# Expert layers in whole fp32 products, weights of each tile from DRAM, and scores ahead of turns

## The chip, the core and the metric

The program runs on one core of one Trainium2 chip. A core has a matrix engine (TensorE, PE in the profile; its weight loads are PEld), a vector engine (DVE), an activation engine (ACT), GpSimd (POOL) and a queue engine (SP). PE writes to PSUM, from which DVE and ACT read. The metric is the device time of one execution in microseconds; lower is better.

## The reference, cut to what matters

Two batches of 2048 tokens of 128 channels go through four layers: a time-mixing layer with a feed-forward part, a ternary feed-forward layer, a state-space layer with a scan over time, and a layer of 8 experts, of which each token takes two. The last one is, for one token x with its normalised vector n:

```
logits = n @ gate_w + gate_b                 # 8 numbers
the two best experts e1, e2, and their shares by softmax
for each of the two: h = silu(n @ w1[e]) * (n @ w3[e])   # 128 -> 512
                     y = h @ w2[e]                       # 512 -> 128
out = x + layernorm(share1 * y1 + share2 * y2)
```

## The kernel before, in words

The program has four phases, one after the other. Every engine has its own stream of instructions, written out by hand; engines wait for one another by semaphores, and no scheduler moves anything. The change touches the third and the fourth phase.

**The state-space phase** (`phase_ssm`) handles 8 tiles of 512 tokens (`body(t, b)`), each in 16 states. For each state DVE multiplies (L1794, 128x1024) and scans (L1781, twice 128x512), POOL multiplies the result by a row of coefficients (`prod`, L1734), and PE adds it up (L1503). Between them this phase also prepares the weights of the experts. There are 12 pieces of 128x1024 numbers. Each is loaded (`weights`, L1387), written by ACT as fp16 (`moe_hi`, L1667), scaled by ACT (L1669), and POOL writes what the fp16 number lacks, as fp16 too (`moe_lo`, L1749).

**The last phase** (`phase_moe`) has four stages.

1. Normalising and scoring. Six of eight groups of 512 tokens are normalised in the phase before; the two late ones here (`centre` L2004, `variance` L2010, `inverse_root`, `normalise` L2322). PE makes each group's scores (`score`, L2018) and turns each group from channels by tokens to tokens by channels (`turn`, L2029), from two fp16 halves, with an identity; ACT and DVE put the rows into SBUF (`put_rows`), and SP stores them in DRAM (`moe_rows`). Scores and turns alternate on PE.
2. Routing. A chain of small instructions on DVE picks the experts (from `logits`, L2346, to `chosen`, L2376), numbers the places (`place`, L2399) and, with PE, turns them round into lists of source rows. The number of the expert of each tile comes near the end of it (`expert`, L2475 to L2481).
3. Experts. The pairs of token and expert are cut into 39 tiles of 256 rows, each tile for one expert. A tile has two units (78 in all). POOL gathers a tile's rows from DRAM (`gather`, L2261, two indirect DMAs), PE turns them (`x_turn`, L2077), DVE copies them (`take_x`, L2491), PE makes the first layer of a unit (`up`, L1998 to L2000: `product` makes three fp16 matmuls for each output of 128x256), ACT takes silu (L2215), DVE multiplies (`hid`, L2507), ACT and DVE split the hidden values into halves (L2201, L2498), and three units later PE makes the second layer (`down`, L2110 to L2112, again three fp16 matmuls). ACT copies the result (`put_y`, L2207), and POOL scatters it to DRAM (L2280, two indirect DMAs).
4. The end: SP loads the results back (`back`), DVE adds the two of each token, POOL, PE and DVE finish the norm and the sum, and SP stores.

In the experts the order on PE is `up(n)`, then at a tile's first unit `x_turn` of the next tile, then `down(n - 3)`. POOL goes tile by tile: scatter of tile i when `y_out` has come, then gather of tile i + 6 when `up` of tile i + 2 is done.

Of the kernel before, what the change touches and what calls it, by code (L numbers as in the profile page):

```python
# [12 lines left out]
P = 128  # L13
# [14 lines left out]
PIECES = E + E // 2  # L28
# [6 lines left out]
for _name, _count in (  # L35
# [11 lines left out]
         "down squaredC varianceC logC rstdC scaledC addedC w_in0 w_in1 w_high w_scaled w_low "  # L47
# [3 lines left out]
def build(nc, xT, vecs, att_w, cv_w, tern_w, hid_w, w3_w, ssm_w, dt_w, moe_w13, moe_w2, gate_w, consts, selectors, iota_c, outT,  # L51
# [3 lines left out]
    with ctx:  # L55
# [74 lines left out]

        G.moe_hi = sb("moe_hi", [P, PIECES, 2 * FFN], F16)
        G.moe_lo = sb("moe_lo", [P, PIECES, 2 * FFN], F16)
# [1165 lines left out]
def phase_ssm(nc, G):  # L1298
# [9 lines left out]
    with mem:  # L1308
# [25 lines left out]
        raw = sb("raw3", [P, 2, 2 * FFN])  # L1334
# [33 lines left out]
        def piece(t, b, k):  # L1368
            return bass.ds((t * B + b) * 2 + k, 1)

        def splits(t):
            return not (isinstance(t, int) and t == NT - 1)

# [7 lines left out]
        def _(sp):  # L1381
            sp.dma_start(G.gatew[:, :], G.gate_w).then_inc(G.gate_loaded, 16)
            w2 = G.moe_w2.rearrange("p (e u) m -> p e (u m)", e=E // 2)
            def weights(i):
                if i >= 2:
                    sp.wait_ge(S["w_low"], i - 1)
                sp.dma_start(raw[:, i % 2, :], G.moe_w13[:, i, :] if i < E else w2[:, i - E, :])\  # L1387
                  .then_inc(S[f"w_in{i % 2}"], 16)
# [13 lines left out]
            for t in range(NT):  # L1402
                for b in range(B):
                    for n in range(DST):
                        spread_C(t, b, n)
                        if t == 0 and b == 0 and n in (1, 2):
                            weights(n - 1)
                        if n in (9, 13):
                            i = at(t, b) * 2 + (9, 13).index(n)
                            if i < PIECES:  # L1410
                                weights(i)
                        if n == 12 and not (t == NT - 1 and b == B - 1):
                            rows_out(*after(t, b))

# [138 lines left out]
        def _(act):  # L1553
# [93 lines left out]
            def body(t, b):  # L1647
                for n in range(DST):
# [16 lines left out]
            def split_weights(t, b, k):  # L1665
                act.wait_ge(S[f"w_in{k}"], at(t, b) * 16)
                nc.scalar.activation(G.moe_hi[:, piece(t, b, k), :].rearrange("p a m -> p (a m)"), raw[:, k, :], ACT.Copy,  # L1667
                                     scale=WS).then_inc(S["w_high"], 1)
                nc.scalar.activation(raw[:, k, :], raw[:, k, :], ACT.Copy, scale=WS).then_inc(S["w_scaled"], 1)  # L1669
# [21 lines left out]
        def _(pool):  # L1691
# [37 lines left out]
            def body(t, b):  # L1729
                for n in range(DST):  # L1730
# [16 lines left out]
            def split_weights(t, b, k):  # L1747
                pool.wait_ge(S["w_scaled"], 2 * at(t, b) - 1 + k)
                nc.gpsimd.tensor_tensor(G.moe_lo[:, piece(t, b, k), :].rearrange("p a m -> p (a m)"), raw[:, k, :],  # L1749
                                        G.moe_hi[:, piece(t, b, k), :].rearrange("p a m -> p (a m)"), ALU.subtract)\  # L1750
                  .then_inc(S["w_low"], 1)
# [89 lines left out]
def phase_moe(nc, G):  # L1841
# [17 lines left out]
    AHEAD, GR, HR, YR = 6, 8, 4, 4  # L1859
# [4 lines left out]
    with mem:  # L1864
        def sb(name, shape, dt=F32):
# [3 lines left out]
        rows = nc.dram_tensor("moe_rows", (P * CHUNKS, 2 * P), F16, kind="Internal").ap()  # L1869
# [10 lines left out]
        ident16 = sb("ident16_4", [P, P], F16)  # L1880
# [7 lines left out]
        xt = sb("xt4", [P, 2, TC, 2 * P], F16)  # L1888
# [24 lines left out]
        past = sb("past4", [1, TILES, E])  # L1913
# [8 lines left out]
        g = sb("g4", [P, GR, 2, 2 * P], F16)  # L1922

        PARTED = GR // 2
        xn_hi, xn_lo = (g[:, k * PARTED:(k + 1) * PARTED, :, :].rearrange("p s r d -> p s (r d)") for k in range(2))
        x16 = sb("x16_4", [P, 2, 2, ROWS], F16)
        silu = sb("silu4", [P, 2, 2 * ROWS])
        hid = sb("hid4", [P, HR, 2 * ROWS])
        hid_hi = sb("hid_hi4", [P, HR, 2 * ROWS], F16)
        hid_lo = sb("hid_lo4", [P, HR, 2 * ROWS], F16)  # L1930
        y = sb("y4", [P, YR, 2, P])
        w13_hi, w13_lo = G.moe_hi[:, 0:E, :], G.moe_lo[:, 0:E, :]
        w2_hi, w2_lo = (w[:, E:, :].rearrange("p u m -> p (u m)").rearrange("p (e m) -> p e m", e=E)
                        for w in (G.moe_hi, G.moe_lo))
# [16 lines left out]
        turns = [w[:, :, :].rearrange("p b n -> p (b n)").rearrange("p (j m) -> p j m", j=TC) for w in (R3, Y)]  # L1951
# [6 lines left out]
                 "centred squared variance logs rstd normed xn_high xn_low scores turned rows_out rows_out2 rows_in0 rows_in1 "  # L1958
# [3 lines left out]
                 "gathered0 gathered1 gathered2 gathered3 gathered4 gathered5 gathered6 gathered7 scattered0 scattered1 scattered2 scattered3 x_turned x_in up silus hidden hid_high hid_low down y_out "  # L1962
# [15 lines left out]
        def _(sp):  # L1978
            by_part = rows.rearrange("(p c) d -> p c d", c=CHUNKS)
            for i in range(GROUPS):  # L1980
                sp.wait_ge(S["rows_out"], i + 1)
                sp.wait_ge(S["rows_out2"], min(i + 1, GROUPS - 2))
# [13 lines left out]
        def _(pe):  # L1996
            def product(out, w_hi, w_lo, x_hi, x_lo, start, stop):
                nc.tensor.matmul(out, w_hi, x_hi, start=start, stop=False)  # L1998
                nc.tensor.matmul(out, w_hi, x_lo, start=False, stop=False)  # L1999
                return nc.tensor.matmul(out, w_lo, x_hi, start=False, stop=stop)  # L2000

# [4 lines left out]
            def variance(i):  # L2006
                pe.wait_ge(S["squared"], late(i) + 1)
                if late(i) >= 1:
                    pe.wait_ge(S["logs"], late(i))
                nc.tensor.matmul(XG[:, 1, :], G.ones, sq[:, i % 2, :], start=True, stop=True)\  # L2010
                  .then_inc(S["variance"], 1)

            def score(i):
                if late(i) >= 0:
                    pe.wait_ge(S["normed"], late(i) + 1)
                for j in range(TC):
                    c = i * TC + j
                    last = nc.tensor.matmul(XG[:, 0, c * E:(c + 1) * E], G.normed[i][:, j * P:(j + 1) * P], G.gatew[:, :],  # L2018
# [3 lines left out]
            def turn(i):  # L2022
                pe.wait_ge(S["xn_low"], i + 1)
                if i >= 2:
                    pe.wait_ge(S["rows_out"], i - 1)
                    pe.wait_ge(S["rows_out2"], i - 1)
                for j in range(TC):
                    for w, half_ in ((0, xn_hi), (1, xn_lo)):
                        last = nc.tensor.matmul(turns[i % 2][:, j, w * P:(w + 1) * P], half_[:, i % PARTED, j * P:(j + 1) * P],  # L2029
                                                ident16[:, :], start=True, stop=True)  # L2030
                last.then_inc(S["turned"], 1)

            centre(EARLY)
            centre(EARLY + 1)
# [3 lines left out]
            for i in range(1, GROUPS):  # L2038
# [15 lines left out]
              .then_inc(S["ranked"], 1)  # L2054
            for q in range(PARTS):
# [15 lines left out]
            def x_turn(i):  # L2071
# [3 lines left out]
                for w in range(2):  # L2075
# [538 lines left out]
```

## Time and profile before

| | |
|---|---|
| median of 3 runs | 1312.6 us (1310.11 to 1313.84) |
| span of the profiled execution | 1360.4 us |
| time shown around that span | none |
| state-space phase, from the first scan to the last | 507 to 990 us |
| scoring and routing | 1007 to 1062 us |
| experts, from the first `up` to the last silu | 1063.3 to 1315.7 us |
| what follows, to the end | 44.7 us |
| PE, DVE, ACT, POOL busy | 81%, 72%, 54%, 54% |

The profile is of one execution, in which the chip also writes a record of every instruction; the median is of runs without it. The profiled execution's span is thus not a run's time: here it is 47.8 us longer than the median. Times of the profile are counted from its first instruction. Matmuls are pipelined: a record's duration is longer than the step from one matmul's start to the next, and only the step tells what one costs in a stream. An fp32 matmul has two records.

### The profile page before, as it was taken

Reading aid. Unit: us, or ns where it says so; the run is one execution under the profiler, and the core shown is the slowest. Engines: PE = TensorE matmul, PEld = TensorE weight load, DVE = VectorE, ACT = ScalarE, POOL = GpSimd, SP = SyncE. Lnnn points to the kernel's source line nnn. Section 1 sums busy time; section 2 is a strip of 40 time slices with the busy share of each in tenths; the row PEclk is TensorE's granted clock in tenths of the full one; section 3 lists DMA queues with packets and bytes.
Section 4 is the critical chain, followed back from the end, with each engine's and each line's share of the span. In section 5 each row is a group of like instructions: output and inputs, shape, how many; then the busy total and the mean of one; then the engine's idle time right before and its main releaser. Section 6 shows DMA issues by size and latency. Waiting matters only on the chain. (4 is left out here: it accounts for less than half of the span.)

```text
span 1360.4 us, 16588 instructions
## 1 busy us (share of the span) xinstructions
PE 1107.5 (81%) x4914; PEld 554.2 (41%) x4914; DVE 986.3 (72%) x1333; ACT 730.8 (54%) x1163; POOL 733.0 (54%) x617
## 2 busy tenths in 40 slices
PE   6564779999999988797988989897883877877863
PEld 2221234444444423243333334332342665666653
DVE  6996775675755449999999999999928644544545
ACT  5765544555555366675766767575533333333444
POOL 0122342331413007898898898979831665656554
PEclk8775899999999988999999999998885989889886
DMA  6000000000000022332323222222101111111115
GB/s 218 0 1 0 0 1 1 0 1 0 0 0 1 0 63 80 90 98 68 107 64 102 88 83 70 76 72 68 57 8 54 37 42 38 42 39 44 36 37 185
DMA packets 32552, 67.07 MB, mean 49 GB/s; under 512 B 5760, under 2 KB 5952, under 8 KB 32256
## 3 DMA queue, kind: packets, MB, share of 16 engines
q1 hardware_dynamic: 27056, 55.16, 12.7%
q0 software_dynamic: 4992, 10.23, 2.9%
q8 instruction: 39, 0.64, 0.2%
q10 hardware_dynamic: 432, 0.76, 0.2%
q14 instruction: 33, 0.27, 0.1%
HBM read 56.57 MB, written 9.57 MB: 49 GB/s over the span
## 5 line engine op out<-in xcount | busy, mean ns | idle before, releaser
L1734 POOL TENSOR_TENSOR prod<-hs,csb 128x1024 f32<-128x1024 f32 x128 | 301.9, 2358 | 142.3 <-DVE hs L1781 141.6
L1781 DVE TENSOR_TENSOR_SCAN hs<-dA,carry,pD 128x512 f32<-128x512 f32 x256 | 313.8, 1267 | 5.6 <-DVE pD L1794 1.2
L1503 PE MATMUL pY<-prod,const 128*128 128x512 f32 x512 | 244.6, 601 | 1.8 <-POOL prod L1734 1.8
L1643 ACT ACTIVATE dA<-dt,negA 128x512 f32<-128x512 f32 x256 | 168.0, 713 | 17.2 <-POOL dt L1703 15.7
L1794 DVE TENSOR_TENSOR pD<-dtu,pD 128x1024 f32<-128x1024 f32 x128 | 155.7, 1216 | 9.2 <-PE pD L1517 9.1
L2507 DVE SCALAR_TENSOR_TENSOR hid<-pR,silu 128x512 f32<-128x512 f32 x78 | 53.8, 689 | 133.0 <-ACT silu L2215 114.6
L1503 PEld LDWEIGHTS pY<-prod,const 128*128 128x128 f32 x512 | 96.7, 192 | 117.7 <-issue 112.7
L2215 ACT ACTIVATE silu<-pR 128x512 f32<-128x512 f32 x78 | 46.5, 596 | 137.0 <-remote 77.2
L2280 POOL DMA_INDIRECT moe_outs<-y,to x78 | 84.0, 1077 | 66.3 <-ACT y L2207 45.6
L2261 POOL DMA_INDIRECT g<-moe_rows,source x78 | 79.6, 1020 | 68.5 <-issue 35.0
L1998 PE MATMUL pR<-x,moe_hi 128*128 128x256 f16 x312 | 92.3, 296 | 14.7 <-DVE x L2491 6.9
L987 ACT ACTIVATE stage<-pR,vec 128x512 f32<-128x512 f32 x64 | 43.9, 688 | 100.1 <-PE pR L687 99.9
L2000 PE MATMUL pR<-x,moe_lo 128*128 128x256 f16 x312 | 91.7, 294 | 5.5 <-issue 5.3
L1999 PE MATMUL pR<-x,moe_hi 128*128 128x256 f16 x312 | 91.8, 294 | 2.3 <-issue 1.9
L1432 PE MATMUL pQ<-xn,convw 128*128 128x512 f32 x112 | 61.6, 676 | 17.4 <-DVE xn L1764 17.4
L2110 PE MATMUL pY<-moe_hi,hid_hi 128*128 x312 | 64.1, 235 | 7.9 <-issue 7.2
L2111 PE MATMUL pY<-moe_lo,hid_hi 128*128 x312 | 63.7, 235 | 4.2 <-issue 4.2
L1037 POOL TENSOR_TENSOR z_lo<-z,z_hi 128x512 f16<-128x512 f32 x8 | 10.6, 1326 | 104.9 <-DVE z_hi L1124 104.9
L429 POOL TENSOR_TENSOR o<-o,rs 128x512 f32<-128x512 f32 x8 | 12.2, 1528 | 101.9 <-DVE o L549 101.9
L2112 PE MATMUL pY<-moe_hi,hid_lo 128*128 x312 | 63.8, 235 | 2.6 <-issue 2.6
L1517 PE MATMUL pD<-split,sel 96*128 96x512 bf16 x128 | 50.0, 391 | 19.0 <-DVE hs L1781 18.4
L1026 POOL TENSOR_TENSOR K_lo<-kstage,K_hi 128x512 f16<-128x512 f32 x24 | 28.8, 1205 | 53.7 <-DVE K_hi L1099 53.7
(422 smaller groups left out, 2591.0 us busy)
## 6 DMA issues: line engine op xcount, KB each, us to landing
csb<-ssm_c SPq DMA_DIRECT2D x128, 256.0 KB, 3.2
raw<-moe_w SPq DMA_DIRECT2D x12, 512.0 KB, 4.9
room<-moe_outs SPq DMA_DIRECT2D x8, 512.0 KB, 7.6
hidw<-hid_w SPq DMA_DIRECT2D x1, 2048.0 KB, 10.1
moe_rows<-xt SPq DMA_DIRECT2D x8, 256.0 KB, 2.0
outT<-X SPq DMA_DIRECT2D x8, 256.0 KB, 2.0
X<-xT SPq DMA_DIRECT2D x3, 512.0 KB, 4.2
g<-moe_rows,source POOLq DMA_INDIRECT x78
```

Of the source, the lines that this page charges most:

```text
L1503: last = nc.tensor.matmul(YB[c][:], G.ident, prod[:, slot(b, n), c, :], start=n == 0, stop=n == DST - 1)
L1643: last = nc.scalar.activation(dA[:, slot(b, n), c, :], dt[:, b, c, :], ACT.Exp, scale=negA[:, c, n:n + 1])
L1734: nc.gpsimd.tensor_tensor(prod[:, slot(b, n), :, :], hs[:, slot(b, n), :, :], csb[:, slot(b, n), :, :].to_broadcast([P, CB, N]), ALU.mult)\
L1781: last = nc.vector.tensor_tensor_scan(hs[:, slot(b, n), c, :], dA[:, slot(b, n), c, :], dBu(n, c), carry[:, b, n, c:c + 1], ALU.mult, ALU.add)
L1794: nc.vector.tensor_tensor(DD[:, (n % 2) * CB:(n % 2) * CB + CB, :], dtu[:, b, :, :], bcastB(n).unsqueeze(1).to_broadcast([P, CB, N]), ALU. ...
L1998: nc.tensor.matmul(out, w_hi, x_hi, start=start, stop=False)
L1999: nc.tensor.matmul(out, w_hi, x_lo, start=False, stop=False)
L2000: return nc.tensor.matmul(out, w_lo, x_hi, start=False, stop=stop)
L2110: nc.tensor.matmul(out, hid_hi[:, n % HR, at], w_hi, start=u == 0 and h == 0 and r == 0, stop=False)
L2112: last = nc.tensor.matmul(out, hid_lo[:, n % HR, at], w_hi, start=False, stop=u == 1 and h == 1 and r == 1)
L2261: nc.gpsimd.indirect_dma_start(g[:, i % GR, r, :], None, rows, bass.IndirectOffsetOnAxis(ap=source[:, 2 * i + r:2 * i + r + 1], axis=0))\
L2280: nc.gpsimd.indirect_dma_start(outs, bass.IndirectOffsetOnAxis(ap=to[:, 2 * i + r:2 * i + r + 1], axis=0), y[:, i % YR, r, :], None).then_ ...
```

## The change

Three edits are made together.

- Experts in fp32. `up` makes one fp32 matmul of each output in place of three fp16 ones, and so does `down`. The gathered rows are 128 fp32 numbers in place of twice 128 fp16 numbers, so that `x_turn` has two fp32 matmuls in place of four fp16 ones. The splits of the hidden values (L2201, L2498), of the weights (L1667, L1669, L1749) and of the normalised groups (L2159, L2255) go, with the scale WS.
- First-layer weights. They no longer lie in SBUF: `w13` is a ring of three slots of 128x1024 fp32 numbers, and SP loads each tile's slot from DRAM at a place given by that tile's expert, once both units of the tile three before are through `up`. The second-layer weights are loaded whole in the state-space phase, in four pieces. For that, `expert` is computed before `place`.
- Scores before turns. PE makes all eight groups' scores first, then the turns of groups 0 to 3, then the two sums over the chosen experts, then the turns of groups 4 to 7. Turns go through three PSUM banks in place of two pairs, and ACT alone puts the rows out.

```
@@ phase_ssm, SP, ACT, POOL
-                if i >= 2:
-                    sp.wait_ge(S["w_low"], i - 1)
-                sp.dma_start(raw[:, i % 2, :], G.moe_w13[:, i, :] if i < E else w2[:, i - E, :])\
-                  .then_inc(S[f"w_in{i % 2}"], 16)
+                sp.dma_start(G.w2[:, i, :], w2[:, i, :]).then_inc(S["experts_in"], 16)
...
-                    if splits(t) and n in (2, 7):
-                        split_weights(t, b, (2, 7).index(n))
...
-                    if splits(t) and n in (4, 8):
-                        split_weights(t, b, (4, 8).index(n))
@@ phase_moe, SP
+            sp.wait_ge(S["expert"], 1)
+            for i in range(TILES):
+                e = sp.value_load(expert[0:1, i:i + 1], min_val=0, max_val=E - 1)
+                if i >= WR:
+                    sp.wait_ge(S["up"], 2 * (i - WR) + 2)
+                sp.dma_start(w13[:, i % WR, :], G.moe_w13[:, bass.ds(e, 1), :].rearrange("p a m -> p (a m)"))\
+                  .then_inc(S[f"w_in{i % WR}"], 16)
@@ phase_moe, PE
+            score(1)
+            for i in range(EARLY, GROUPS):
+                variance(i)
+            for i in range(2, GROUPS):
                 score(i)
-                if 2 <= i < 4:
-                    variance(EARLY + i - 2)
-                turn(i - 1)
-            turn(GROUPS - 1)
-            pe.wait_ge(S["rows_out"], GROUPS)
+            for i in range(GROUPS // 2):
+                turn(i)
...
+            for i in range(GROUPS // 2, GROUPS):
+                turn(i)
+            pe.wait_ge(S["rows_out"], GROUPS)
...
-            def up(n, e):
+            def up(n):
                 i, u = divmod(n, 2)
                 if u == 0:
+                    pe.wait_ge(S[f"w_in{i % WR}"], 16 * (i // WR + 1))
                     pe.wait_ge(S["x_in"], i + 1)
...
-                        last = product(out[:, u, h * ROWS:(h + 1) * ROWS], of_expert(w13_hi, e, m), of_expert(w13_lo, e, m),
-                                       x16[:, i % 2, 0, :], x16[:, i % 2, 1, :], True, True)
+                        last = nc.tensor.matmul(out[:, u, h * ROWS:(h + 1) * ROWS], w13[:, i % WR, m], xe[:, i % 2, :],
+                                                start=True, stop=True)
...
             def down(n, e):
                 i, u = divmod(n, 2)
-                pe.wait_ge(S["hid_low"], n + 1)
+                pe.wait_ge(S["hidden"], n + 1)
...
-                        nc.tensor.matmul(out, hid_hi[:, n % HR, at], w_hi, start=u == 0 and h == 0 and r == 0, stop=False)
-                        nc.tensor.matmul(out, hid_hi[:, n % HR, at], w_lo, start=False, stop=False)
-                        last = nc.tensor.matmul(out, hid_lo[:, n % HR, at], w_hi,
-                                                start=False, stop=u == 1 and h == 1 and r == 1)
+                        last = nc.tensor.matmul(out, hid[:, n % HR, at], w_out, start=u == 0 and h == 0 and r == 0,
+                                                stop=u == 1 and h == 1 and r == 1)
```

Two places show what the edits do to the streams. The first is PE in the experts, before, from the last of four outputs of an `up` to the first of four of a `down` (`moe_hi` and `moe_lo` are the weights' halves, `TENSOR_LOAD` reads the expert's number):

```order
L1998 ISA
L1998 MATMUL pR_4<-x_4,moe_hi 128x256
L1999 MATMUL pR_4<-x_4,moe_hi 128x256
L2000 REGISTER_ALU
L2000 MATMUL pR_4<-x_4,moe_lo 128x256
L2117 TENSOR_LOAD expert
L2117 ISA x2
L2077 MATMUL pX<-ident_4,g 128x128 x4
L2110 ISA
L2110 MATMUL pY<-moe_hi,hid_hi 128x128
L2111 REGISTER_ALU
L2111 MATMUL pY<-moe_lo,hid_hi 128x128
```

The same place of the changed kernel, here a whole `up`, turn and `down` (`w_4` is the ring for L2058 and the second-layer weights for L2074):

```order
L2058 MATMUL pR_4<-xe,w_4 128x256 x4
L2079 TENSOR_LOAD expert
L2079 ISA x2
L2040 MATMUL pX<-const,g 128x128 x2
L2074 ISA
L2074 MATMUL pY<-w_4,hid 128x128 x2
L2074 ISA
L2074 MATMUL pY<-w_4,hid 128x128 x2
```

A unit has 12 matmuls of 128x256 and 12 of 128x128 before, and 4 and 4 now, each of them fp32.

The second place is PE in the first stage of the last phase, before (`gatew` marks scores, `ident_4` turns, `sq` variances):

```order
L2018 MATMUL pX<-gatew,convw 128x8 x8
L2029 MATMUL pR_4<-ident_4,g 128x128 x8
L2018 MATMUL pX<-gatew,h 128x8 x4
L2010 MATMUL pX<-sq,const 128x512
L2029 MATMUL pY<-ident_4,g 128x128 x8
L2018 MATMUL pX<-gatew,h 128x8 x4
L2010 MATMUL pX<-sq,const 128x512
L2029 MATMUL pR_4<-ident_4,g 128x128 x8
L2018 MATMUL pX<-gatew,sgate 128x8 x4
L2029 MATMUL pY<-ident_4,g 128x128 x8
```

And the same place now, to the sums over the chosen experts (`const` with 128x128 marks turns):

```order
L1982 MATMUL pX<-gatew,convw 128x8 x8
L1974 MATMUL pX<-sq,const 128x512
L1974 MATMUL pY<-sq,const 128x512
L1982 MATMUL pX<-gatew,h 128x8 x8
L1982 MATMUL pX<-gatew,sgate 128x8 x8
L1982 MATMUL pX<-gatew,hid 128x8 x8
L1990 MATMUL pR_4<-const,convw 128x128 x8
L1990 MATMUL pY<-const,h 128x128 x4
L1990 MATMUL pR_4<-const,h 128x128 x4
L2010 MATMUL pX<-chosen,later 128x256
```

Four turns stand between the last score and the sum over the chosen experts, where before six turns of eight fp16 matmuls stood among the scores and two behind them. On DVE three instructions (`past`, `expert_f`, `expert`) now stand ahead of `place`, and none between the two lists.

## Rows read from the trace of the kernel before

**Rows 1.** The page: its first line.
```profile
span 1360.4 us, 16588 instructions
```
**Rows 2.** Windows: length, busy time of PE, PEld, DVE, ACT, POOL, clock, DMA share, GB/s.
```profile
700.00:760.00 60.00, 53.30 (x126) 21.42 (x125) 58.09 (x51) 40.83 (x61) 52.81 (x41) 0.98 0.27 87
1063.00:1315.60 252.60, 202.07 (x1990) 163.74 (x1990) 119.66 (x192) 95.45 (x192) 149.18 (x144) 0.89 0.15 39
```
**Rows 3.** Order of time in the experts: start, duration, instruction, idle before it.
```profile
1109.11 0.27 PE L1998 MATMUL pR<-x,moe_hi 128*128 128x256 f16 x1
1109.22 0.27 PE L1999 MATMUL pR<-x,moe_hi 128*128 128x256 f16 x1
...
1110.39 0.27 PE L2000 MATMUL pR<-x,moe_lo 128*128 128x256 f16 x1
...
1113.36 0.60 ACT L2215 ACTIVATE silu<-pR 128x512 f32<-128x512 f32 x1 [4.05 <-remote]
...
1113.60 0.22 PE L2110 MATMUL pY<-moe_hi,hid_hi 128*128 x1
1113.66 0.22 PE L2111 MATMUL pY<-moe_lo,hid_hi 128*128 x1
```
**Rows 4.** POOL in the experts, by lines: count, busy, mean ns, idle before by releaser.
```profile
L2280 POOL DMA_INDIRECT moe_outs<-y,to x73 | 79.2, 1085 | 63.5 <-ACT y L2207 44.1 <-issue 15.9 <-PE pR L2000 2.4
L2261 POOL DMA_INDIRECT g<-moe_rows,source x72 | 71.0, 986 | 40.5 <-issue 33.5 <-PE pR L2000 6.4 <-ACT y L2207 0.6
```
**Rows 5.** Waits in the state-space phase (total, times, longest), and one line there.
```profile
DVE pD L1794 <- PE pD L1517: 9.1, 17, 2.2
DVE hs L1781 <- DVE pD L1794: 1.2, 4, 0.5
L1749 POOL TENSOR_TENSOR moe_lo<-raw,moe_hi 128x1024 f32 (+1 forms) x12 | 25.6, 2130 | 0.0
```
**Rows 6.** Scoring and routing, in order of time.
```profile
1009.39 1.95 PE L2018 MATMUL pX<-gatew,convw 128*128 128x8 f32 x16
1024.33 1.82 PE L2018 MATMUL pX<-gatew,convw 128*128 128x8 f32 x8
1026.19 0.42 DVE L2346 TENSOR_TENSOR logits<-pX,vec 128x256 f32<-128x256 f32 x1 [0.20 <-PE pX L2018]
1033.01 0.37 PE L2049 MATMUL pX<-chosen,later 128*128 128x256 f16 x1 [5.14 <-DVE chosen L2376]
1059.58 0.47 DVE L2475 TENSOR_TENSOR past<-tiles_to,lane_f 1x312 f32<-1x312 f32 x1
1063.25 0.28 PE L1998 MATMUL pR<-x,moe_hi 128*128 128x256 f16 x1 [1.21 <-DVE x L2491]
```
**Rows 7.** Steps at full clock: fp16 of 512 columns; fp32 loads; fp32 of 128 columns.
```profile
299.70 0.38 PE L686 MATMUL pR<-A_lo,hid_hi 128*128 128x512 f16 x1
299.92 0.38 PE L687 MATMUL pR<-A_hi,hid_lo 128*128 128x512 f16 x1
...
957.61 0.19 PEld L1509 LDWEIGHTS pY<-h,skip 128*128 128x128 f32 x1 [0.24 <-issue]
958.04 0.19 PEld L1509 LDWEIGHTS pY<-h,skip 128*128 128x128 f32 x1 [0.24 <-issue]
...
1353.19 1.16 PE L2138 MATMUL pR<-const,sq 128*128 128x128 f32 x8 [0.58 <-POOL sq L2294]
```
**Rows 8.** The first microseconds of the experts, PE in order of time.
```profile
1065.29 0.42 PE L1998 MATMUL pR<-x,moe_hi 128*128 128x256 f16 x1
1065.50 0.42 PE L1999 MATMUL pR<-x,moe_hi 128*128 128x256 f16 x1
```
**Rows 9.** The last silu and the last scatter.
```profile
1315.07 0.60 ACT L2215 ACTIVATE silu<-pR 128x512 f32<-128x512 f32 x1
1323.32 0.97 POOL L2280 DMA_INDIRECT moe_outs<-y,to  x1 [0.30 <-issue]
```
**Rows 10.** The page's DMA issues: count, size, median time to landing.
```profile
raw<-moe_w SPq DMA_DIRECT2D x12, 512.0 KB, 4.9
```

More of the change, by code:

```diff
@@ L1366, in landed @@
             return 16 * (t * (B * DST // RING) + (b * DST + n) // RING + 1)
[L1368 to L1372, printed above, removed]
         def is_final(t):
@@ L1996, in _ @@
         def _(pe):
[L1997 to L2000, printed above, removed]
             def centre(i):
@@ L2007, in variance @@
                 pe.wait_ge(S["squared"], late(i) + 1)
-                if late(i) >= 1:
-                    pe.wait_ge(S["logs"], late(i))
-                nc.tensor.matmul(XG[:, 1, :], G.ones, sq[:, i % 2, :], start=True, stop=True)\
+                nc.tensor.matmul(late_variance[late(i)], G.ones, sq[:, i % 2, :], start=True, stop=True)\
                   .then_inc(S["variance"], 1)
@@ L2022, in turn @@
             def turn(i):
[L2023 to L2026, printed above, removed]
+                if i >= TR:
+                    pe.wait_ge(S["rows_out"], i - TR + 1)
                 for j in range(TC):
-                    for w, half_ in ((0, xn_hi), (1, xn_lo)):
-                        last = nc.tensor.matmul(turns[i % 2][:, j, w * P:(w + 1) * P], half_[:, i % PARTED, j * P:(j + 1) * P],
-                                                ident16[:, :], start=True, stop=True)
+                    last = nc.tensor.matmul(turns[i % TR][:, j, :], normed[i][:, j * P:(j + 1) * P], G.ident,
+                                            start=True, stop=True)
                 last.then_inc(S["turned"], 1)
-            centre(EARLY)
-            centre(EARLY + 1)
+            for i in range(EARLY, GROUPS):
+                centre(i)
             pe.wait_ge(S["consts"], 1)
@@ L2074, in x_turn @@
                     pe.wait_ge(S["x_in"], i - 1)
-                for w in range(2):
-                    for r in range(2):
-                        last = nc.tensor.matmul(XG[:, i % 2, (2 * w + r) * P:(2 * w + r + 1) * P],
-                                                g[:, i % GR, r, w * P:(w + 1) * P], ident16[:, :], start=True, stop=True)
+                for r in range(2):
+                    last = nc.tensor.matmul(XG[:, i % 2, r * P:(r + 1) * P], g[:, i % GR, r, :], G.ident,
+                                            start=True, stop=True)
                 last.then_inc(S["x_turned"], 1)
@@ L2164, in put_rows @@
                     act.wait_ge(S[f"rows_in{i % 2}"], 16 * (i // 2))
-                most = TC // 2 if i < GROUPS - 2 else TC
-                nc.scalar.activation(xt[:, i % 2, 0:most, :], turns[i % 2][:, 0:most, :], ACT.Copy)\
-                  .then_inc(S["rows_out"], 1)
+                nc.scalar.activation(xt[:, i % 2, :, :], turns[i % TR], ACT.Copy).then_inc(S["rows_out"], 1)
             act.preload_act_table_set("natural_log_exp_and_others")
-            high(0)
-            high(1)
-            square(EARLY)
-            square(EARLY + 1)
-            for i in range(2, GROUPS):
-                high(i)
-                if i < 4:
-                    inverse_root(EARLY + i - 2)
-                put_rows(i - 2)
-            put_rows(GROUPS - 2)
-            put_rows(GROUPS - 1)
+            for i in range(EARLY, GROUPS):
+                square(i)
+            for i in range(EARLY, GROUPS):
+                inverse_root(i)
+            for i in range(GROUPS):
+                put_rows(i)
             act.wait_ge(S["gap"], 1)
@@ L2195, in _ @@
                   .then_inc(S["hot_part"], 1)
-            def hid_high(n):
-                act.wait_ge(S["hidden"], n + 1)
-                if n >= HR:
-                    act.wait_ge(S["down"], n - HR + 1)
-                nc.scalar.activation(hid_hi[:, n % HR, :], hid[:, n % HR, :], ACT.Copy).then_inc(S["hid_high"], 1)
             def put_y(i):
```

138 lines of the change are left out of this document (42 added, 96 removed).

## The prediction

> **What bounds the kernel now.** I read the page's span first, then the windows of each stage, then the experts in order of time. The profiled execution spans 1360.4 us [rows 1]; the runs have a median of 1312.6. A span cannot be longer than the run that contains it, so the profiled execution is a slower one, by at least 47.8 us, and the first question is where.
>
> In the state-space phase DVE is busy 58.09 of 60 us [rows 2]: it bounds the phase, and runs cannot be faster there. In the experts no engine is that full. PE shows 202 of 252.6 us at a clock of 0.89 [rows 2], but its real work is less. In an undisturbed stretch an fp16 matmul of 256 columns starts 0.11 us after the last, one of 128 columns 0.0555 us [rows 3]. A tile has 24 of the first, 24 of the second and 4 turning ones: 2.62 + 1.33 + 0.22 = 4.17 us, for 39 tiles 163 us. POOL issues four indirect DMAs a tile. The 145 in the stage took 150.2 us and the gaps before them that wait for nothing shown 49.4 us, together 199.6, or 1.38 each and 5.5 us a tile; it waited another 52.9 us for ACT and PE (44.1 + 2.4 + 6.4) [rows 4]. So POOL paces the stage, and something else adds 53 us.
>
> What that is stands in [rows 3]: the last matmul of an `up` starts at 1110.39, and the silu that it releases starts at 1113.36, after 4.05 us of waiting for a releaser that the profile cannot name; the stream of matmuls with its steps of 0.055 us is back at 1113.60. PE stood still there with nothing to wait for. These pauses come back through the experts and nowhere else, where PE starts more instructions in a microsecond than in any other stage. Their cost by POOL's waits, at most 52.9 us, is what the profiled execution has too much (at least 47.8). I take it that the runs have no such pauses: their experts take about 200 to 205 us, paced by POOL, and their span is near 1360.4 - 52.9 = 1307.5, which leaves 5 us of the median outside the span (between 0 and some 10, since some of POOL's waits at the stage's start and end are real).
>
> **The change part by part.** The sum is made on the profiled execution's own clock, for a changed kernel without pauses, and 5 us are added for a run.
>
> State-space phase. POOL loses 25.6 us [rows 5] and ACT 24 copies, all beside DVE. DVE sat idle for 9.1 us before its multiplications and 1.2 before its scans, and most of the first wait for PE's broadcast, which stays. I take 1.5 us of gain; the ends are 0 and 3. The cover is DVE's own 3.6 us a state; nothing is added that could use it up. Four loads of 512 KB replace twelve.
>
> Scores. Eight scores and two variances now run without turns between them. Two scores took 1.95 us at full clock, one 1.82 at half [rows 6], both with a tail that a row of them has once: 0.9 and 1.65 each. From 1009.4, where the first begins [rows 6], two scores take 1.9, the variances (two fp32 records of 0.43 each, or twice that) 1.7 to 3.4 and six scores 5.3 to 10: the last ends between 1018.3 and 1024.7 where it ended at 1026.0. I take 1022, since both clocks occur in the stretch: 4 us. The routing chain from `logits` to `chosen` [rows 6] covers the first four turns (each 8 fp32 records of 0.11 or 0.21, 3.6 to 6.8 us against 6.8); beyond that a turn would delay the sum by under 1 us. The other four stand behind it, while DVE makes the lists for 15 us. The expert's number, three instructions of which the first takes 0.47 [rows 6] and all together 1.1, moves from behind the first list, where it delayed nothing but the first `x_turn`, to the front of the chain: it costs 1.1. Together the first `up` starts 1.5 + 4.3 - 1.1 = 4.7 us earlier, at 1058.5 [rows 6]; the ends are 0.5 and 9.
>
> Experts. An fp32 matmul of 256 columns is two records. Such a record lies between half of an fp32 record of 512 columns, 0.43 / 2 = 0.215, and the step of 0.22 that an fp16 matmul of 512 columns has [rows 7]; I take 0.216. One of 128 columns lies between 0.43 / 4 = 0.1075 and 1.16 / 8 = 0.145 (eight of them in 1.16 us, with the start and the tail of the last in it) [rows 7]; I take 0.112, near the 0.11 of the fp16 matmul of 256 columns, which streams as much. A tile has 8 fp32 matmuls in `up` (16 records), 8 in `down` and 2 turning ones (20 records): 16 x 0.216 + 20 x 0.112 = 5.70 us against 4.17. With the low values 5.59, with the high ones 6.42. For 39 tiles: 222, between 218 and 250.
>
> That is above POOL's 5.5 a tile, whose DMAs are the same in number and bytes (256 rows of 512 bytes), above DVE (two products and a copy, under 2 us) and above ACT (1.6). PE becomes the bound by 0.2 us a tile. Its waits are covered: `up(n)` needs the hidden product of n - 2, one silu and one product (0.60 and 0.69) behind `up(n - 2)`, with 2.6 us of PE's work between.
>
> At the start the clock is at its lower level, with steps of 0.21 for 0.11 [rows 8], for about 3.3 us: 1.7 us. Two us are allowed for seams, an estimate. PE then ends its last `down` at 1058.5 + 222 + 1.7 + 2 = 1284.2, and the last `up` four downs (0.9 each) before, at 1280.6. The last silu starts 0.3 later. From there to the last scatter it was 8.3 us [rows 9]; the hidden split is gone, one `down` is longer, so 7 to 8.3; I take 7. From it to the end it was 37.1 us [rows 1, 9], untouched. The span becomes 1280.9 + 7 + 37.1 = 1325.0, **35 us under the profiled span of before**, and a run takes 5 more: **1330 us, 1.3% slower than 1312.6**. The same change thus shortens the profile and lengthens the run.
>
> The ring. SP's load of tile i waits for both ups of tile i - 3; nothing but the next loads is queued behind it on SP until the last scatter. The only rows of such a load are those of the state-space phase, 4.9 us [rows 10]. The period is at least (landing + 5) / 3, for 4.9 us 3.3, so a landing must pass 12 us before PE waits. With 512 KB more a tile the traffic is 39 + 92 = 131 GB/s.
>
> **The rivals.**
>
> Pauses in the runs too (the other side). If PE's pauses are a property of its stream and not of the profiled execution, the runs have them, the missing 47.8 us lie spread elsewhere, and fp32, which starts half as many instructions in a microsecond, removes them: 1312.6 - 35 = 1278. For it: nothing in the trace names the cause. Against it: DVE and PE run at the same steps through every other stage, so there is no place for 48 us. It decides from 18 us of pauses in the runs on.
>
> A part of them. If 14 to 22 us of pauses are real, or the experts are paced by POOL before and after, the two kernels come out level, at 1309 to 1316.
>
> Weights late. If gathers, scatters and SP's loads get in each other's way and a load lands after 20 us, a tile takes 8.3 us: 1330 + 39 x 2.6 = 1431. Landing times under load are not in this trace; 4.9 was measured at 87 GB/s [rows 2, 10].
>
> Weight loads uncovered. An fp32 load takes 0.19 us [rows 7], more than the 0.112 of a record of 128 columns. If it is not hidden, the 20 short records cost 0.19 each: 39 x 20 x 0.078 = 61 us, 1391 us. Against it: eight such records took 1.16 us, 0.145 each at most. The Trainium skill, TensorE: Matmul & The Clock Gate, Weight-path perf modes, says that the fast weight load is off for fp32, which speaks for it; the trace agrees on the load (0.19 for fp32) but not on a stream bound by it.
>
> **How the numbers follow.** The forecast has 0.67, with its own range of 1317 to 1348 (low: 218 us, 9 us of gain, no time outside the span and no seams, 1314; high: a step of 0.13 for short records, 8 seam us, 10 outside). Pauses in the runs 0.15, level 0.10, weights late 0.05, loads uncovered 0.03. A measurement of this kernel can tell 0.3% from no change, 4 us. Slower is 0.67 + 0.05 + 0.03 = 0.75, the same 0.09, faster 0.16. The range runs from the level cases to the forecast's upper end, 1307 to 1348; it leaves out most of the first rival and the last two.
>
> **What would show it.** In the profile after: records of `up` 0.216 us apart and of `down` 0.112, no idle PE before silu for an unnamed releaser, a stage of 222 to 228 us at a clock near 1, POOL waiting a little each tile; `logits` at 1020 to 1024; DVE's scans unchanged; a span near 1325. Wrong if `up` waits for the ring, if pauses persist, or if the run is not above its own profile's span.

## The result, and the profile after

| | before | changed |
|---|---|---|
| median of the runs | 1311.9 us (1310.11 to 1313.84, 4 runs) | 1321.7 us (1320.22 to 1326.05, 4 runs) |
| ratio changed / before | | 1.0079, 95% interval 1.0055 to 1.0103 |
| span of the profiled execution | 1360.4 us | 1321.1 us |

The changed kernel is 0.8% slower, some 10 us, while its profiled execution is 39 us shorter than the one shown of before. That execution of before was out of line. Every run after it lists a span of its own, 1.8 us under its time, and 52 more runs of the kernel before (42 beside the experiments and the ten of experiment 1) took 1307.1 to 1316.1 us. So the runs and the profiled executions are of one kind, and what was said above, that the runs differ by having no records, doesn't hold. A second profile of the kernel before spans 1309.8 us; "before" below is that one, where rows of it are shown.

The experts, in windows: length, busy time (and records) of PE, PEld, DVE, ACT and POOL, granted clock, DMA share, GB/s. First the changed kernel, then before, in its second profile.

```profile
1063.00:1263.00 200.00, 200.00 (x1262) 185.36 (x1261) 61.16 (x108) 55.41 (x105) 136.75 (x140) 1.00 0.51 139
```
```profile
1063.00:1263.00 200.00, 167.00 (x1959) 147.72 (x1957) 123.66 (x199) 96.79 (x187) 150.26 (x145) 0.98 0.19 49
```

PE is busy for all of the 200 us where it had holes of 33 us. DVE and ACT have about half of their work left. POOL is busy for 14 us less: it issues 140 indirect DMAs in place of 145, since it now waits, and each is shorter (the last section has their lengths). Its waits in the changed kernel, and before (total, times, longest; "issue" is no wait for another engine):

```profile
POOL moe_outs L2213 <- ACT y L2148: 22.9, 27, 0.9
POOL g L2194 <- issue: 20.4, 67, 0.3
POOL moe_outs L2213 <- issue: 13.3, 37, 1.6
POOL g L2194 <- PE pR L2058: 7.8, 3, 3.5
```
```profile
POOL moe_outs L2280 <- issue: 20.7, 68, 0.3
POOL g L2261 <- issue: 18.3, 60, 0.3
POOL g L2261 <- PE pR L2000: 7.7, 6, 4.1
POOL g L2261 <- ACT y L2207: 2.1, 7, 0.3
```

The 7.8 and 7.7 belong to the first tiles. After them POOL waited for next to nothing before, and waits 0.85 us a tile now. In order of time, from one tile's scatter to the next one's (the second scatter and two gathers lie between), first of the changed kernel, then of before:

```profile
1124.24 0.99 POOL L2213 DMA_INDIRECT moe_outs<-y,to  x1 [0.85 <-ACT y L2148]
...
1128.13 0.96 POOL L2194 DMA_INDIRECT g<-moe_rows,source  x1 [0.30 <-issue]
1129.93 0.99 POOL L2213 DMA_INDIRECT moe_outs<-y,to  x1 [0.85 <-ACT y L2148]
```
```profile
1121.38 1.00 POOL L2280 DMA_INDIRECT moe_outs<-y,to  x1 [0.31 <-issue]
...
1126.52 1.00 POOL L2280 DMA_INDIRECT moe_outs<-y,to  x1 [0.30 <-issue]
```

From scatter to scatter it is 5.69 us after and 5.14 before. And PE, a tile of the changed kernel in order of time (x8 is four fp32 matmuls of two records each):

```profile
1119.82 1.89 PE L2058 MATMUL pR<-xe,w 128*128 128x256 f32 x8
1121.55 0.61 PE L2040 MATMUL pX<-const,g 128*128 128x128 f32 x4
1121.99 1.06 PE L2074 MATMUL pY<-w,hid 128*128 x8
1122.88 1.89 PE L2058 MATMUL pR<-xe,w 128*128 128x256 f32 x8
1124.61 1.05 PE L2074 MATMUL pY<-w,hid 128*128 x8
1125.50 0.81 PE L2058 MATMUL pR<-xe,w 128*128 128x256 f32 x3
```

The starts give the prices: (1121.55 - 1119.82) / 8 = 0.216 us a record of 256 columns, (1121.99 - 1121.55) / 4 = 0.110 and (1122.88 - 1121.99) / 8 = 0.111 for 128, and 1125.50 - 1119.82 = 5.68 us a tile.

The places of [rows 6] and [rows 9] in the changed kernel, in order of time:

```profile
1009.39 1.96 PE L1970 MATMUL pR<-X,const 128*128 128x512 f32 x4 [2.47 <-PEq L159]
...
1021.64 3.76 PE L1990 MATMUL pR<-const,convw 128*128 128x128 f32 x16
...
1028.60 0.28 PE L2010 MATMUL pX<-chosen,later 128*128 128x256 f16 x1 [1.37 <-DVE chosen L2297]
```
```profile
1021.83 0.42 DVE L2267 TENSOR_TENSOR logits<-pX,vec 128x256 f32<-128x256 f32 x1 [4.29 <-PE pX L1982]
...
1028.11 0.42 DVE L2297 TENSOR_TENSOR chosen<-picks 128x256 f16<-128x256 f32 x1
```
```profile
1059.87 1.96 PE L2058 MATMUL pR<-xe,w 128*128 128x256 f32 x8 [2.07 <-DVE xe L2412]
```
```profile
1277.91 0.60 ACT L2156 ACTIVATE silu<-pR 128x512 f32<-128x512 f32 x1 [1.35 <-PE pR L2058]
...
1284.77 0.96 POOL L2213 DMA_INDIRECT moe_outs<-y,to  x1 [0.30 <-issue]
```

Cut at these places, the two programs compare as follows (us):

| stretch | before | changed |
|---|---|---|
| start to the first scan | 507.1, 506.6 | 509.2 |
| first scan to the phase's first `centre` | 500.2, 500.2 | 500.2 |
| `centre` to the first `up` | 55.9, 58.7 (two more profiles of the same code: 56.2, 57.1) | 50.5 |
| first `up` to the start of the last silu | 199.6 (251.8 in the first profile) | 218.0 |
| from there to the end | 44.8 | 43.2 |

The first stretch has the same code in every kernel of this study and lies between 506.2 and 512.1 in their profiles; it is scatter. What is left is -6.5 (57.0, the mean of four, to 50.5) + 18.4 - 1.6 = +10.3 us, and the ratio of the runs gives 0.0079 x 1311.9 = +10.4.

### The profile page after: what moved, and what is told of

It is laid out like the page before. It is cut to its first block and busy times, and to the rows that moved or that the text cites. A ratio compares the mean times of both kernels' runs of the same rounds, so it can differ in the third digit from the quotient of the medians.

```text
span 1321.1 us, 14376 instructions
## 1 busy us (share of the span) xinstructions
PE 1129.0 (85%) x4290; PEld 598.7 (45%) x4290; DVE 926.8 (70%) x1248; ACT 667.6 (51%) x1053; POOL 691.0 (52%) x597
## 5 line engine op out<-in xcount | busy, mean ns | idle before, releaser
L2421 DVE TENSOR_TENSOR hid<-pR,silu 128x512 f32<-128x512 f32 x78 | 53.9, 691 | 153.0 <-ACT silu L2156 153.0
L2058 PE MATMUL pR<-xe,w 128*128 128x256 f32 x624 | 147.5, 380 | 2.1 <-DVE xe L2412 2.1
L2058 PEld LDWEIGHTS pR<-xe,w 128*128 128x128 f32 x624 | 112.7, 191 | 14.3 <-issue 2.2
L2213 POOL DMA_INDIRECT moe_outs<-y,to x78 | 77.0, 987 | 51.0 <-ACT y L2148 35.3
L2074 PE MATMUL pY<-w,hid 128*128 x624 | 81.8, 275 | 0.0
L2074 PEld LDWEIGHTS pY<-w,hid 128*128 128x128 f32 x624 | 78.7, 192 | 2.0
L1417 PE MATMUL pQ<-xn,convw 128*128 128x512 f32 x112 | 61.6, 676 | 17.4 <-DVE xn L1733 17.4
L1030 POOL TENSOR_TENSOR A_lo<-stage,A_hi 128x512 f16<-128x512 f32 x32 | 37.3, 1170 | 26.0 <-DVE A_hi L1205 26.0
L683 PE MATMUL pR<-A_hi,hid_hi 128*128 128x512 f16 x128 | 48.5, 379 | 1.2 <-issue 0.6
```

Source lines behind the costliest of these rows:

```text
L1417: last = nc.tensor.matmul(Q[c][:], convw[:, c, k, :], xn[b][:, k:k + N], start=k == 0, stop=k == TAPS - 1)
L2058: last = nc.tensor.matmul(out[:, u, h * ROWS:(h + 1) * ROWS], w13[:, i % WR, m], xe[:, i % 2, :], start=True, stop=True)
L2074: last = nc.tensor.matmul(out, hid[:, n % HR, at], w_out, start=u == 0 and h == 0 and r == 0, stop=u == 1 and h == 1 and r == 1)
L2213: nc.gpsimd.indirect_dma_start(outs, bass.IndirectOffsetOnAxis(ap=to[:, 2 * i + r:2 * i + r + 1], axis=0), y[:, i % YR, r, :], None).then_ ...
L2421: nc.vector.tensor_tensor(hid[:, n % HR, :], R3[:, u, :], silu[:, u, :], ALU.mult).then_inc(S["hidden"], 1)
```

## The experiments

Times are medians; the ratio is to the kernel before, run beside it on the same chip (1310.9, 1311.9 and 1313.5 us in the three groups).

**1. The kernel before once more.** No edit. 

> The kernel before, unchanged, with a profile of its own. My theory: the first profile's 1360.4 us belong to that one execution (or to profiled ones of this kernel alone); the timed runs take about 1312 us with spans some 2 us shorter, near 1310, and nothing in the experts stands still in them. If the pauses belong to every profiled execution of this kernel, its profile spans 1350 to 1370 again; if they belong to one execution, it spans 1308 to 1315 and the experts take 199 to 203 us. Rival: the pauses are in the runs too; then a profile that spans about 1310 still shows some 50 us of silu waiting for an unnamed releaser.

1310.5 us, ratio 0.9995 (0.9980 to 1.0011); its profile spans 1309.8. The experts take 199.6 us, from the first of these two rows to the second:

```profile
1065.47 0.28 PE L1998 MATMUL pR<-x,moe_hi 128*128 128x256 f16 x1 [2.11 <-DVE x L2491]
```
```profile
1265.05 0.60 ACT L2215 ACTIVATE silu<-pR 128x512 f32<-128x512 f32 x1 [0.59 <-PE pR L2000]
```

No silu waits for an unnamed releaser, where the first profile had 18 such waits, 77.2 us in all. ACT's waits there are these.

```profile
ACT silu L2215 <- PE pR L2000: 76.1, 77, 6.4
ACT y L2207 <- PE pY L2112: 29.6, 24, 2.8
```

The pauses of [rows 3] are of the first profile alone, and the rival that put them into the runs is dead.

**2. The kernel before with less PE work.**

```
-                nc.tensor.matmul(out, w_hi, x_lo, start=False, stop=False)
-                return nc.tensor.matmul(out, w_lo, x_hi, start=False, stop=stop)
+                return nc.tensor.matmul(out, w_hi, x_lo, start=False, stop=stop)
...
-                        nc.tensor.matmul(out, hid_hi[:, n % HR, at], w_lo, start=False, stop=False)
```

> The kernel before with the third product of halves left out of every output of the experts (its result lacks that term); PE's work falls from 4.17 to 2.85 us a tile. My theory: POOL's four indirect DMAs set the pace of a tile before (about 5.2 us), so nothing changes: 1308 to 1313 us. Rival, PE or its pauses set the pace: 39 tiles x 1.32 = 51 us off, 1260.

1307.9 us, ratio 0.9976 (0.9961 to 0.9992). A third of PE's products, 51 us of them at full clock, are worth 3. The granted clock from 1063 to 1262 us fell from 0.98 to 0.85, which takes back a part of the 51 us. For most of the rest PE waits longer than before (total, times, longest), first here, then before:

```profile
PE pX L2076 <- DMA g<-moe_rows,source: 54.2, 29, 4.1
```
```profile
PE pX L2077 <- DMA g<-moe_rows,source: 30.2, 24, 2.4
```

What PE waits for is a gather's landing, and the gathers come out of POOL's full queue.

**3 and 4. One gather of two left out, before and changed.** The edit is the same in both.

```
-                for r in range(2):
+                for r in range(2 if i < GR else 1):
                     nc.gpsimd.indirect_dma_start(
                         g[:, i % GR, r, :], None, rows,
...
-                pe.wait_ge(S[f"gathered{i % GR}"], 32 * (i // GR + 1))
+                pe.wait_ge(S[f"gathered{i % GR}"], 32 + 16 * (i // GR))
```

> The kernel before without the second of the two gathers of each tile from tile 8 on (31 indirect DMAs fewer; those tiles use stale rows in half of their places). My theory: POOL's pace falls from 5.2 to about 3.8 us a tile, PE's 4.17 becomes the bound, 31 x 1.0 = 31 us off: 1281. Rival, PE sets the pace already: 0 to 3 us off.

> The changed kernel without the second gather of each tile from tile 8 on (31 indirect DMAs fewer, stale rows in half of those tiles), the same edit that took 37 us off the kernel before. My theory: PE is the bound here, 0 to 3 us off: 1319 to 1322. Rival, POOL still sets the pace as it did before: 25 us or more off, under 1297.

Before: 1273.8 us, ratio 0.9716 (0.9687 to 0.9745), 37 us less; the experts take 163.3 us in place of 199.6. Changed: 1320.1 us, ratio 1.0073 (1.0047 to 1.0099) where the changed kernel has 1.0079; the experts take 218.0 us as they did. POOL's waits there, in the changed kernel with one gather less:

```profile
POOL moe_outs L2213 <- ACT y L2148: 62.0, 29, 2.1
```

The same work taken away is worth 37 us in one kernel and nothing in the other. This is the plainest proof of the pair of bounds: POOL before, PE after. The two also give the price of fp32 with POOL out of the way: 218.0 against 163.3 us of experts, 54.7, where the change shows 18.4.

**5. The changed kernel with less PE work.**

```
-                for h in range(2):
+                for h in range(1 if i >= 1 and u == 1 else 2):
                     for out, at in ((R1, 0), (R3, FFN)):
```

> The changed kernel with 2 of the 8 fp32 matmuls of a tile's first layer left out from tile 1 on (stale numbers in a quarter of the hidden units). That is 4 records x 0.216 = 0.865 us a tile and 33 us for 38 tiles. My theory: PE's tile of 5.6 us falls to 4.75, but POOL's pace of 5.2 us then holds: 38 x 0.45 = 17 us off, 1304. Rival, POOL is no floor at 5.2: all 33 us off, 1289.

1296.6 us, ratio 0.9893 (0.9863 to 0.9924), 25 us under the changed kernel, between the two numbers. POOL's pace is back at 5.14 us:

```profile
1184.09 1.00 POOL L2213 DMA_INDIRECT moe_outs<-y,to  x1 [0.30 <-issue]
...
1189.23 1.00 POOL L2213 DMA_INDIRECT moe_outs<-y,to  x1 [0.30 <-issue]
```

So there is a floor, but I had used it for all tiles. Once the scatters have begun, POOL's stream has 33 rounds of two scatters and two gathers and six rounds of scatters alone, since six tiles are gathered ahead. 33 x (5.69 - 5.14) + 5 x 0.865 = 22.5 us; the experts got shorter by 24.6 (193.4). This sum was made after the run, and nothing else tests it.

**6. No loads into the ring.** It is filled once; the other 36 loads are left out.

```
-            for i in range(TILES):
+            for i in range(WR):
                 e = sp.value_load(expert[0:1, i:i + 1], min_val=0, max_val=E - 1)
-                if i >= WR:
-                    sp.wait_ge(S["up"], 2 * (i - WR) + 2)
```

> The changed kernel with the ring filled once and then left (36 loads of 512 KB left out, stale weights). My theory: the loads cost nothing, PE never waits for one: the same time within 2 us, 1320 to 1323. Rival, the loads' traffic slows gathers and scatters or PE's start of a tile: 5 us or more off.

1321.3 us, ratio 1.0072 (1.0045 to 1.0098); experts 218.0 us. The loads cost nothing that the runs can tell.

**7. A ring of two.** `WR` is 2 in place of 3. 

> The changed kernel with two slots in the ring in place of three. From the end of a tile's last up to the first up of the tile two on, 0.9 + 5.7 = 6.6 us pass, and a load lands 3.6 to 4.6 us after its issue. My theory: it still fits, 0 to 1 us slower: 1320 to 1323. Rival: the wait for `up`, the load's issue and the landing's word to PE take the other 2 us and PE waits at each tile: 5 us or more slower, over 1326.

1322.8 us, ratio 1.0085 (1.0062 to 1.0108); experts 218.2 us. PE's only waits from 1050 to 1275 us are at the start:

```profile
PE pR L2058 <- DVE xe L2412: 2.1, 1, 2.1
PE pY L2031 <- ACT room L2141: 0.4, 1, 0.4
```

Loads landed 3.5 to 4.8 us after their issue. Two slots do.

**8. Scores ahead of turns alone.** The kernel before with this part of the change, the halves kept. PE's order, as in the changed kernel but for one more wait, for `logs`:

```
             score(0)
-            for i in range(1, GROUPS):
-                score(i)
-                if 2 <= i < 4:
-                    variance(EARLY + i - 2)
-                turn(i - 1)
-            turn(GROUPS - 1)
-            pe.wait_ge(S["rows_out"], GROUPS)
+            score(1)
+            for i in range(EARLY, GROUPS):
+                variance(i)
+            for i in range(2, GROUPS):
+                score(i)
+            pe.wait_ge(S["logs"], GROUPS - EARLY)
+            for i in range(GROUPS // 2):
+                turn(i)
```

> The kernel before with one of the three edits alone: scores of all groups ahead of the turns, ACT alone putting out the rows, everything else in halves as before, the expert's number where it was. In the changed kernel the last score came 6.4 us sooner after the phase's start and the moved expert's number cost 1.0. My theory: the experts start 5 to 6 us earlier and nothing gives it back: 1306 us, ratio 0.9955. Rival: the splits into halves (8 on ACT, 8 on POOL) pace the turns, ACT's whole rows come late, the lists wait for the turns' banks, and the gain is 0 to 2 us: 1310 to 1312.

1309.1 us, ratio 0.9986 (0.9974 to 0.9998): 2 us, not 5 to 6. `logits` comes 12.7 us after the phase's start, as planned (18.8 to 20.6 before), but from there to `chosen` it is 9.6 us in place of 6.2. In order of time:

```profile
1024.61 1.16 POOL L2256 TENSOR_TENSOR g<-sgate,g 128x512 f16<-128x512 f32 x1 [4.80 <-ACT g L2161]
1024.76 1.28 DVE L2347 TENSOR_TENSOR picks<-rev,first 128x256 f32<-128x256 f32 x1
...
1026.04 1.15 POOL L2256 TENSOR_TENSOR g<-sgate,g 128x512 f16<-128x512 f32 x1 [0.28 <-ACT g L2161]
1026.08 1.40 DVE L2350 SCALAR_TENSOR_TENSOR logits<-picks,logits 128x256 f32<-128x256 f32 x1
...
1027.51 0.59 DVE L2353 TENSOR_REDUCE best<-logits 128x32 f32<-128x256 f32 x1
...
1027.70 1.16 POOL L2256 TENSOR_TENSOR g<-hid,g 128x512 f16<-128x512 f32 x1 [0.51 <-ACT g L2161]
...
1028.83 0.41 DVE L2356 TENSOR_TENSOR equal<-logits,best 128x256 f32<-128x256 f32 x1
```

Three DVE products of 128x256 start while one of POOL's subtractions runs. They take 1.28, 1.40 and 1.35 us in place of 0.42, and the two shown end 0.27 and 0.29 us after that subtraction. The maximum at 1027.51, which reads one operand, keeps its 0.59 beside the subtraction of 1027.70, and the product at 1028.83, between two subtractions, its 0.41. The Trainium skill, SBUF — State Buffer, SBUF: two separate sides, has this as a port pair that DVE and GpSimd share, held for a whole instruction; a DVE instruction with two operands in SBUF takes part against a GpSimd one that reads SBUF. The trace agrees, in what slows down and in what doesn't. In the first profile of before, POOL's last subtraction ends 0.3 us ahead of the chain; with the scores moved ahead, the chain runs beside POOL's splits.

**9. The same without the splits.** Rows in DRAM whole, as in the changed kernel, turned in fp32, and split into halves by DVE once per tile, behind the turn; the experts keep three fp16 products.

```
-                nc.vector.tensor_copy(x16[:, i % 2, :, :].rearrange("p w s -> p (w s)"), XG[:, i % 2, :])\
+                nc.vector.tensor_copy(x16[:, i % 2, 0, :], XG[:, i % 2, 0:ROWS]).then_inc(S["x_high"], 1)
+                dve.wait_ge(S["x_high"], i + 1)
+                nc.vector.tensor_tensor(x16[:, i % 2, 1, :], XG[:, i % 2, 0:ROWS], x16[:, i % 2, 0, :], ALU.subtract)\
                   .then_inc(S["x_in"], 1)
```

> The kernel before with scores ahead of turns, and with whole fp32 rows in DRAM: the groups aren't split into halves; each tile's gathered rows are turned in fp32 and split by DVE after the turn (two instructions in place of one), and the experts stay at three fp16 products. In the run with scores ahead and halves kept, the last score came 6.8 us sooner but the routing chain took 9.6 us in place of 6.2, with DVE's 0.42 us instructions at 1.3 to 1.4 while POOL's 1.16 us subtractions ran. My theory: these two engines get in each other's way there, and without the subtractions the chain takes 6.2 us again and the gain is 6 us: 1305 us. PE's tile grows by 0.22 to 4.4 us, still under POOL's pace. Rival: the chain was late for the picks' own reasons, or the extra split on DVE costs in the experts: 1308 to 1311.

1303.9 us, ratio 0.9936 (0.9916 to 0.9956), 8 us under before. The chain takes 6.3 us again:

```profile
1020.52 0.43 DVE L2312 TENSOR_TENSOR logits<-pX,vec 128x256 f32<-128x256 f32 x1 [4.46 <-PE pX L2015]
...
1023.16 0.42 DVE L2323 TENSOR_TENSOR picks<-rev,first 128x256 f32<-128x256 f32 x1
1023.62 0.42 DVE L2326 SCALAR_TENSOR_TENSOR logits<-picks,logits 128x256 f32<-128x256 f32 x1
...
1026.82 0.42 DVE L2342 TENSOR_TENSOR chosen<-picks 128x256 f16<-128x256 f32 x1
```

The first `up` is 50.7 us after the phase's start (57.0 before), and the experts take 199.7 us, as before. This version has the change's gain without its price. The trace accounts for 6.3 us; the interval reaches from 6 to 11.

**10 and 11. POOL's first gathers into its idle time, without and with the change.** The edit is made to the version of experiment 9 and to the changed kernel.

```
-    AHEAD, GR, HR, YR = 6, 8, 4, 4
+    AHEAD, GR, HR, YR = 8, 8, 4, 4
...
-                if i >= AHEAD // 2:
-                    pool.wait_ge(S["up"], 2 * (i - AHEAD // 2) + 1)
```

> The version with scores ahead, fp32 rows and three fp16 products, with POOL's first gathers moved into its idle time: eight tiles gathered ahead in place of six, and the first ones no longer held back for the matrix engine's first units. POOL stood idle there for 8.6 us (5.0, 1.6 and 2.0). My theory: POOL sets the pace of these experts, so the four indirect DMAs of two tiles that leave its paced part are worth 5.1 us, and the first scatter, which waits for the first result, comes at most 0.7 us sooner: 5 to 6 us off 1303.9, 1298. Rival: the tile's latency through the engines holds the start, and PE's tile of 4.4 us fills the rest: 0 to 2 us off.

> The changed kernel with the same edit of POOL's first gathers. My theory: PE sets the pace here, so what takes work out of POOL's paced part is worth nothing: 1320 to 1323 us. Rival: POOL is still a partner in the pace, 2 to 5 us off.

To the version of experiment 9: 1299.3 us, ratio 0.9896 (0.9872 to 0.9919), 14 us under before and the best of this study. The two versions ran in different groups: by their medians 4.6 us of it is this edit's, by their ratios 5.2, and each ratio is known to some 3 us. The trace shows less of it. The experts shrink by 5.8 us (193.9), but part comes back: it is 47.6 us from the last silu to the end, in place of 44.6, since POOL's backlog of scatters is still there. That leaves 2.8, so the 5 to 6 expected are not shown by the stages. (The profiled run took 1305.0, the longest of its five.) POOL, in order of time, its first scatter and its last:

```profile
1074.73 1.23 POOL L2255 DMA_INDIRECT moe_outs<-y,to  x1 [1.59 <-ACT y L2190]
...
1266.34 0.97 POOL L2255 DMA_INDIRECT moe_outs<-y,to  x1 [0.30 <-issue]
```

Of these 192 us it waits 2.2 for others. To the changed kernel: 1322.0 us, ratio 1.0078 (1.0051 to 1.0104), no gain; its experts take the same 218.0 us.

## Why the prediction was right

It said 1330 us and slower, for the reason that the runs show: PE's tile in fp32 is longer than what POOL needs for a tile, and POOL had hidden PE's work before. The size was too large. As a difference the forecast was +17.4 us (1330 - 1312.6) and +10 came. By stages it was +23.5 in the experts (222.4 against 251.8 - 52.9 = 198.9), -4.7 up to the first `up` and -1.2 at the end; measured were +18.4, -6.5 and -1.6. All three errors point the same way.

- **What bounds.** Right, and from the wrong profile: the inference that [rows 1] had 47.8 us too much, that these lay in PE's pauses, and that the runs had none, was confirmed by experiment 1 (span 1309.8; I had 1307.5). Experts of before: 200 to 205 us said, 199.6 measured. That the number fits so well is in part luck: the sum had 49.4 us of POOL's issue gaps and next to no real waits, and the second profile has 39.9 us of gaps and 10.1 of waits, most of them at the first tiles. What stopped PE in that one execution stays open; no later profile has it.
- **POOL's pace.** "5.5 us a tile" was mis-sized; POOL's rows in the disturbed profile had longer idle time counted as issue. It is 5.14 us where nothing is in the way and 5.28 on average: from the first scatter to the last, 144 indirect DMAs took 150.1 us and their issue gaps 39.9. The difference to PE is thus 0.4 to 0.55 us a tile, not "0.2", and this is where most of the 18.4 us of the experts come from. The prediction's "0.2 us a tile" and its sum don't fit each other: 39 x 0.2 is 8, and the sum had 23.5. The sum is the better of the two: POOL issues only 145 of its 156 indirect DMAs in the stage, the work of 36 tiles, while PE goes through `up` for all 39.
- **PE's tile.** "16 x 0.216 + 20 x 0.112 = 5.70" is right to 0.02. That the low end came from half and a quarter of an fp32 matmul's step of 512 columns shows how such a price can be had without a row of its own.
- **Half clock and seams.** "1.7 us" and "two us" for the seams were 0. From the first `up` to the last silu there are 78 ups, 38 turns and 74 downs before the last up: 78 x 8 x 0.216 + 38 x 4 x 0.111 + 74 x 8 x 0.1115 = 217.7, and it took 218.0; I had 222.4. The first up's eight records took 1.96 us, against 1.89 at full clock. The half clock of [rows 8] was of the first profile too: in the second, before's first records stand 0.11 us apart.
- **The state-space phase.** "1.5 us of gain" was 0. Its length is 500.2 us in both, and DVE's two waits are what they were, 9.1 and 1.2 us. It was 498.6 in three profiles of the second group, changed and not, and 500.2 in that group's fourth, so it scatters by itself.
- **Scores.** "4.3" was 6.4: `logits` comes 12.4 us after the first `centre` and came 18.8 after it. (The text had 4 us for it, the sum 4.3.) The mis-sized term is the clock: I took the middle between full and half for two variances and six scores, 10.7 us; they took 8.6, the variances and four of the scores at a granted clock of 1.00 and only the last two scores at 0.53. The moved expert's number costs 0.9 (from `chosen` to the first gather 20.9 against 20.0); "1.1" was said. With the front's scatter of +2.0 the first `up` came at 1059.9; 1058.5 was said.
- **The end.** 44.1 us said, 43.2 measured.
- **Outside the span.** "5 us" was 1.8. It had been worked out as a remainder, which took up the errors of the rest.

In sum -4.4 (experts) + 1.4 (first up) - 0.9 (end) - 3.2 (outside) = -7.1, from 1330 to the profiled run's 1322.9; the median is 1.2 below it.

**The rivals.** Pauses in the runs: fell with experiment 1. Level cases: the POOL-paced one came nearest, for POOL hid 36 of the 55 us that fp32 costs (experiments 3 and 4). Weights late: not by far, even two slots are enough. Weight loads uncovered: no. The loads take 0.19 us and the records follow each other in 0.111, as this row of the changed kernel shows (duration min/median/max in ns):

```profile
L2074 PEld LDWEIGHTS pY<-w,hid x571: 190/192/193, 1067.5 to 1270.0; 128*128 128x128 f32 x191
```

Loads of 0.19 us at steps of 0.111 overlap. Had each load been waited for, the prediction's sum gives 1391 us, and the trace decides against that. The Trainium skill (TensorE: Matmul & The Clock Gate, Weight-path perf modes) says that fast weight load is off for fp32. It doesn't say that such loads bound a stream, and in this one they didn't.

## What to carry to other kernels

Before you price a faster or slower engine, find which engine's stream has no holes, and test it by taking work from each in turn: 31 indirect DMAs were worth 37 us in one kernel and nothing in its sibling. A profiled execution that is longer than every run holds something that isn't the kernel's; take its idle time out before anything is learnt from it, and take a second profile. And a part of a change can be worth having when the whole isn't: scores ahead of turns and whole rows in DRAM gave 8 us with the fp16 products kept.

## What the runs showed of the hardware

- One execution of the 57 on record of the kernel before had PE standing still for microseconds at a time in the experts, 50 us in all, with no releaser that the profile could name [rows 3].
- An fp32 matmul of 128x128x256 costs 0.432 us (two records of 0.216) and the same in three fp16 products 0.328 (3 x 0.109); for 128 columns 0.223 against 0.167. In PE's time fp32 is thus a third dearer than three products.
- POOL's indirect DMAs are shorter beside the fp32 experts, where DVE has no splits left: 971 and 990 ns on average against 1027 and 1061, by lines of POOL in the experts of the changed kernel and of before (busy, mean ns of one, idle before):

```profile
L2194 POOL DMA_INDIRECT g<-moe_rows,source x72 | 69.9, 971 | 28.8 <-issue 20.4 <-PE pR L2058 7.8 <-ACT y L2148 0.6
L2213 POOL DMA_INDIRECT moe_outs<-y,to x66 | 65.3, 990 | 36.8 <-ACT y L2148 22.9 <-issue 13.3 <-PE pR L2058 0.6
```
```profile
L2261 POOL DMA_INDIRECT g<-moe_rows,source x73 | 75.0, 1027 | 28.1 <-issue 18.3 <-PE pR L2000 7.7 <-ACT y L2207 2.1
L2280 POOL DMA_INDIRECT moe_outs<-y,to x69 | 73.2, 1061 | 21.0 <-issue 20.7 <-PE pR L2000 0.3
```

That DVE's splits are the cause was argued from experiment 8, and not tried: no run took them out and left the rest as it was.
